# Expert layer in half precision parts: the down products accumulate both weight parts into one set of 128 columns

## What is computed

```python
xt = m.reshape(-1, Dd)                       # 8192 tokens x 128, normalised
probs = jax.nn.softmax(xt @ Wg, axis=-1)     # 8 experts
wts, idx = jax.lax.top_k(probs, 2)
wts = wts / jnp.sum(wts, axis=-1, keepdims=True)
h1 = jax.nn.gelu(jnp.einsum('td,edf->etf', xt, W1) + b1[:, None, :])   # 128 -> 512
ye = jnp.einsum('etf,efd->etd', h1, W2) + b2[:, None, :]               # 512 -> 128
sel = ye[idx, jnp.arange(T)[:, None], :]
moe_out = jnp.sum(wts[..., None] * sel, axis=1)
```

## Time and profile before

| | us |
|---|---|
| median of 3 runs | 1005.7 |
| lowest and highest of them | 1004.23, 1015.59 |
| the profiled execution | 1008.4 |
| its span, first to last instruction | 1006.6 |

### The profile page before, as it was taken

The page is one execution under the profiler, slowest core; times in us unless marked ns, Lnnn a source line. Parts: engine busy times, 40 slices in busy tenths (PEclk is TensorE's granted clock), DMA queues, the critical chain, the costliest instruction groups (busy, mean ns, idle before and its releaser), DMA issues.

```text
span 1006.6 us, 25427 instructions
## 1 busy us (share of the span) xinstructions
PE 776.2 (77%) x8366; PEld 476.2 (47%) x8367; DVE 805.4 (80%) x1600; ACT 585.4 (58%) x1198; POOL 532.5 (53%) x669
## 2 busy tenths in 40 slices
PE   2678776789989898989788888849989999993000
PEld 2445454324445443434344444338878888873000
DVE  7789989788887989898988885168999888888412
ACT  6755468557776777777667778325545555551000
POOL 8600378601254735341233778737887076665775
PEclk9999999869998999999889999559999999997555
DMA  8740015311111111111011120115544455544422
GB/s 196 277 149 1 1 71 187 126 41 56 51 46 42 55 55 55 54 34 34 18 33 57 54 63 26 45 37 119 134 120 130 90 127 131 133 116 111 124 74 73
DMA packets 132073, 84.19 MB, mean 84 GB/s; under 512 B 54520, under 2 KB 117628, under 8 KB 131982
## 3 DMA queue, kind: packets, MB, share of 16 engines
q1 hardware_dynamic: 123790, 66.20, 23.0%
q0 software_dynamic: 8192, 16.79, 6.3%
HBM read 30.25 MB, written 41.94 MB: 72 GB/s over the span
## 4 chain that ended last, share of the span: by engine, by line
PE 59%; POOL 10%; issue 9%; DVE 9%; ACT 8%; DMA 1%; ACTq 0%; POOLq 0%; DVEq 0%; SPq 0%
PE bank L1358 54%; ACT arena L870 5%; POOL Z L771 3%; POOL HT L771 3%; PE bank L1545 2%; PE bank L1362 1%; DVE arena L1053 1%; POOL xh L500 1%; POOL rr L496 1%; ACT arena L779 1%; PE bank L1552 1%; DVE QK L1314 1%; DVE mom L972 1%; DVE arena L1122 1%; DVE Z L1037 1%
## 5 line engine op out<-in xcount | busy, mean ns | idle before, releaser
L1122 DVE TENSOR_REDUCE arena<-bank 128x2 f32<-128x512 f32 x512 | 329.5, 685 | 45.3 <-PE bank L1358 41.1
L870 ACT ACTIVATE arena<-bank 128x512 f32<-128x512 f32 x512 | 288.2, 596 | 113.7 <-PE bank L1358 111.8
L1358 PE MATMUL bank<-w2p,QK 128*128 x1280 | 216.8, 246 | 1.4 <-DVE arena L1321 1.4
L1358 PE MATMUL bank<-QK 32*128 32x256 f16 (+1 forms) x2048 | 179.2, 284 | 45.9 <-ACT arena L870 28.3
L945 ACT ACTIVATE arena<-bank,b1s 128x256 f32<-128x256 f32 x320 | 125.3, 475 | 107.9 <-PE bank L1358 99.1
L1358 PE MATMUL bank<-arena,w1h 128*128 128x256 f16 x640 | 166.6, 277 | 5.3 <-DVE arena L1321 2.3
L698 POOL DMA_INDIRECT expert_in<-HT,idx x128 | 134.1, 1047 | 69.0 <-issue 28.5
L1358 PE MATMUL bank<-arena,VA 128*32 128x256 f32 x2048 | 145.3, 404 | 0.7 <-ACT arena L870 0.7
L1358 PEld LDWEIGHTS bank<-QK 32*128 32x128 f16 (+1 forms) x2048 | 51.2, 93 | 169.1 <-ACT arena L870 133.6
L1358 PEld LDWEIGHTS bank<-w2p,QK 128*128 128x128 f16 x1280 | 123.8, 98 | 11.0 <-issue 1.7
L1316 DVE TENSOR_TENSOR QK<-arena,QK 128x1024 f16<-128x1024 f32 x80 | 98.0, 1225 | 2.7
(11 more groups left out here) (158 smaller groups left out, 1148.3 us busy)
## 6 DMA issues: line engine op xcount, KB each, us to landing
QK<-qk_parts SPq DMA_DIRECT2D x96, 128.0 KB, 2.6
expert_in<-arena SPq DMA_DIRECT2D x40, 256.0 KB, 3.2
expert_out<-arena SPq DMA_DIRECT2D x80, 128.0 KB
qk_parts<-arena SPq DMA_DIRECT2D x16, 512.0 KB, 2.8
X<-x SPq DMA_DIRECT2D x8, 512.0 KB, 5.9
wst<-w SPq DMA_DIRECT2D x16, 256.0 KB, 2.8
out<-arena SPq DMA_DIRECT2D x16, 256.0 KB, 2.7
expert_in<-HT,idx POOLq DMA_INDIRECT x128
```

What stands on the lines that cost most here:

```text
L870: nc.scalar.activation(PT[t % 8], bank[3 + t % 2][:, :], ACT.Exp, scale=DH ** -0.5)\
L1122: V.tensor_reduce(nmax[n % 2][:, :, 4 * j + g], bank[u % 3][:, :].rearrange("p (q t) -> p q t", q=2), AX.X, ALU.max, negate=True).then_inc ...
L1358: return nc.tensor.matmul(dst, lhsT, rhs, start=start, stop=stop)
```

## The change

`down` splits each product with 256 columns in two with 128: the high part of the weights and then the low part, both into the same 128 columns of the bank. The bias goes into those columns too. The block's result then stands complete in 256 columns of the bank (128 for each half of the tokens), in place of 512, and `y_out` has nothing to add: it becomes a copy, and it moves from DVE to ACT, ahead of the gelu in each body. A block now has 26 down products in place of 18. The pieces of the interleaving stay 18, since the two products of a chunk's high hidden part make one piece.

```diff
@@ block.scalar
             def experts(b, q):
+                if exists(b - 1):
+                    y_out(b - 1, (q + 1) % 2)
                 if exists(b + 2):
                     gelu(b + 2, q % 2)
 
+            def y_out(b, s):
+                act.wait_ge(down_done, b + 1)
+                used(act, yb_out[s], 8 * (b - s))
+                copy(YB[s], bank[6 + s][:, 0:2 * P].rearrange("p (h d) -> p h d", h=2)).then_inc(yb_ready, 1)
+
             blocks(act, -2, experts, second_part=lambda: act.wait_ge(tab_ready, 2))
+            y_out(NBLK - 1, 1)
@@ block.vector
-            def y_out(b, s):
-                dve.wait_ge(down_done, b + 1)
-                used(dve, yb_out[s], 8 * (b - s))
-                V.tensor_reduce(YB[s], bank[6 + s][:, :].rearrange("p (h k d) -> p h d k", h=2, k=2), AX.X, ALU.add)                    .then_inc(yb_ready, 1)
-
             def experts(b, q):
-                if exists(b - 1):
-                    y_out(b - 1, (q + 1) % 2)
                 if exists(b + 2):
                     split(b + 2, (q + 2) % 4)
 
             blocks(dve, -2, experts)
-            y_out(NBLK - 1, 1)
@@ block.tensor
             def down(b, q, e):
                 for h in range(2):
-                    dst = bank[6 + q % 2][:, 2 * P * h:2 * P * h + 2 * P]
+                    dst = bank[6 + q % 2][:, P * h:P * h + P]
                     for c in range(FC):
                         x = slice(BS * c + P * h, BS * c + P * h + P)
-                        w = w2p[:, bass.ds(e, 1), c, :, :].rearrange("p a k d -> p (a k d)")
-                        mm(dst, GH[q][:, x], w, start=c == 0, stop=False)
+                        whi, wlo = (w2p[:, bass.ds(e, 1), c, k, :].rearrange("p a d -> p (a d)") for k in range(2))
+                        mm(dst, GH[q][:, x], whi, start=c == 0, stop=False)
+                        mm(dst, GH[q][:, x], wlo, start=False, stop=False)
                         yield
-                        w = w2p[:, bass.ds(e, 1), c, 0, :].rearrange("p a d -> p (a d)")
-                        mm(dst[:, 0:P], GL[q][:, x], w, start=False, stop=False)
+                        mm(dst, GL[q][:, x], whi, start=False, stop=False)
                         yield
-                    last = mm(dst[:, P:2 * P], ones16[:, :], b2h[:, bass.ds(e, 1), :].rearrange("p a d -> p (a d)"),
+                    last = mm(dst, ones16[:, :], b2h[:, bass.ds(e, 1), :].rearrange("p a d -> p (a d)"),
                               start=False)
```

## The result

The changed kernel takes 1049.6 us (median of 4 runs, 1045.04 to 1051.32), the kernel before, run beside it, 1006.6: a ratio of 1.041, 95% interval 1.037 to 1.046. It is slower by 43 us where 33 were forecast.

What follows compares the result with a forecast made beforehand. PE's sequencer was taken as the bound, 11.43 us an iteration rising to 13.5. Loop +27.6, first iteration +2.1 and blocks outside +3.5 gave +33.2 us on the median 1005.7: 1039 us, range 1022 to 1060.

Steps and rivals of the forecast that it cites:

- What bounds the kernel: Experts' loop: PE's sequencer, not the array, sets the 11.43 us an iteration, despite PE busy at 98%.
- Address operations: Experts' down blocks: a second address per chunk, 16 more operations an iteration at 124 ns, 1.98 us.
- 27.6: Experts' loop: 16 iterations go from 188.4 to 216.0 us, at 13.5 us each.
- Products and weight loads: Experts' down blocks: issuing eight more products and weight loads a block costs 0.1 us an iteration; array columns cost 0.
- The 81 ns: Experts' down products: the skill's figure per 128-column load and product pair; 3.41 us a block, an estimate giving 1050.
- DVE's relief: Experts: DVE loses a 683 ns reduce a block, but this shows as nothing at 13.5 us an iteration.
- evenly, also where POOL adds its tensors: Experts' loop: sign of a right forecast, branches 13.5 us apart even during POOL's additions.
- ACT: Experts: ACT gains the copy, 1.57 to 2.02 us a block; gelu 0.5 us late, within slack, cost 0.
- Rival C: Experts: gelu behind the copy comes too late each block; +36 us, 1042, or up to 1060 on the forecast; chance 0.04.
- PE idle released by ACT: Experts' loop: the profile sign that would show ACT's late gelu binding; no size given.
- 2.1: Experts: the us added by the loop's first iteration.
- 3.5: Experts: the us added by twelve blocks outside the loop, taken below 6.0 because some wait on their own pipeline.

Runs made afterwards that it cites:

- experiment 7: The kernel before, with PE loading an expert's number without the range check behind it: 997.0 us, ratio 0.989.
- Experiment 9: The changed kernel with the copy on DVE and the low half's product at the high half's address (26 products), second chip: 1008.1 us, ratio 1.002.
- experiment 11: The changed kernel, copy on ACT, but ACT loads the expert's number ahead of the copy's wait, second chip: 1037.7 us, ratio 1.031.
- experiment 10: The kernel before with 18 down products, but four more operand addresses a block, second chip: 1040.9 us, ratio 1.033.
- 12: The changed kernel with the copy on DVE and no range check behind PE's load of the expert's number: 1016.5 us, ratio 1.009.
- experiment 1: The kernel before with 18 down products, but four more operand addresses a block, first chip: ratio 1.0175.
- experiment 2: The changed kernel with the copy on DVE and the low half's product at the high half's address (26 products), first chip: ratio 1.004.

## Why the prediction was right, and where it fell short

- *What bounds the kernel.* Right. The count of sequencer instructions filled the iteration: taking eight of them away and shortening four (experiment 7) brought it down to the array's time, adding sixteen lengthened it by 1.9 us. PE's 98% did not say that the array was the limit. The records of the 324 instructions sum to 21.4 us, not 20.5, so what follows each is 75 ns and not 78.
- *Address operations.* Right: 16 more an iteration, 0.120 us each where 0.124 was taken. Over the loop with its POOL stretch they cost 25.9 us, where 27.6 with the issue of the products was forecast.
- *Products and weight loads.* I took 0.1 us an iteration for issuing them; it is 0.01. The array's own cost was put at 0, and is. The 81 ns of the Trainium skill (TensorE: Matmul & The Clock Gate, Back-to-back issue gap) would by the prediction's estimate have made a block 3.41 us. Experiment 9 has 2.86 us with 26 such products, and three of them start within 0.17 us, never more in a row.
- *DVE's relief.* Right that it shows as nothing: with the copy on ACT (its load first) or the reduce left on DVE the loop takes 213.9 and 214.3 us (experiments 11 and 10). The sign "evenly, also where POOL adds its tensors" did not come true for the change as made, 14.4 us against 13.77; it holds on the second chip as long as the gelu is in time.
- *ACT.* This is the step that failed: "The gelu is then 0.5 us late; PE asks for it only a block and more later", cost 0. The gelu starts 1.1 us behind the last up product, for 0.14 before, since the load of the expert's number is issued behind the copy's wait. I had named the gelu as what is queued there, and not the load ahead of it. And PE's sequencer, which does the asking, runs ahead of the array (it began its wait at 837.77, and the array fell idle at 838.06), so that "a block and more" was less for it. It measured 0.43 us an iteration in the steady part and 1.0 in the first eight, 11.3 us in all. Rival C had this mechanism, a chance of 0.04 and a price of up to 36 us. Its sign, PE idle released by ACT, did not appear: the idle time is put down to "issue", and only the sequencer's wait at line 338 shows the cause. On top of the forecast its 36 us would be 1075, not the 1060 that it states.
- *The sum.* 27.6 + 2.1 + 3.5 = 33.2 against 43.0. In the traces the loop has 36.8 for 27.6, of which 11.3 are ACT's order, and outside it 4.5 + 2.9 = 7.4 for 5.6. The time lies in the stated range of 1022 to 1060, but the sum is 10 us low for want of the ACT term. Without ACT's order (experiment 11) the change is at 1.031, 31.6 us; the loop has 213.9 - 188.4 = 25.5 for 27.6 there, and 5.8 stand outside it for 5.6, so the other terms were right one by one.

## What to carry to other kernels

An engine that the profile shows at 98% can be fed at its limit or be limited by its feeder: count the sequencer's instructions, and look whether the idle time of the engine is put down to "issue" and comes once per iteration. Where operands are addressed through a register, splitting a product can cost an address operation for each new offset, here 0.120 us, where the product itself cost next to nothing. And when work moves to another engine with a wait, everything that stands behind the wait in that stream moves with it, register loads too: place these ahead of it (here worth 11.3 us).

## What was not expected of the hardware

- The cost of a register operation on PE's sequencer is nearly three times its recorded duration, however many products stand around it: 0.120 us for 46 ns with 18 products a block (experiment 10), and (13.34 - 11.45) / 16 = 0.118 us with 26 (experiments 11 and 9), while thirty-two products with their weight loads cost 0.01 us together.
- The range check behind a register load is dear: without it (four loads an iteration; two sequencer instructions fewer for each, and one shorter) an iteration of before fell by 0.46 us, down to the array's time, and one of the change by 1.2 us, where the array was not yet the limit (experiments 7 and 12).
- The kernel before takes 1058 us on one chip and 1006 to 1009 on another, and the same four addresses a block cost 1.8% there where they cost 3.3% here (experiments 1 and 10). The cause is open. What the traces show is that more than half of the difference lies ahead of the experts (24 of 40.7 us for the kernel of experiment 1), and that PE's sequencer waits for late gelus there (up to 1205 ns against 185 in experiment 2).
